# Attention weights transposed 64 rows at a time into two banks, with the first stage's order written anew

## What is computed

```python
x = x + xcond(layernorm(x), ctx, ctx, tau, delta, L0 weights)   # 16 heads of 32, 77 keys a batch
x = x + ffn(layernorm(x), ...)       # 512 -> 64, sum over relu(s*W1+b1)*W2, -> 512
x = x + xcond(layernorm(x), ctx, ctx, tau, delta, L1 weights)
x = x + routed_attention(x, ...)     # local windows, a router, attention of routed tokens

# xcond, for each batch and head
scores = q @ k.T * tau + delta       # 2048 x 77
a      = softmax(scale * scores)
out    = (a @ v) @ Wo.T + bo
```

## Time and profile before

| | us |
|---|---|
| median of 3 runs (3152.45 to 3153.17) | 3153.17 |
| the profiled execution | 3140.98 |
| its span, first to last instruction | 3139.1 |
| mean granted clock of PE, share of full speed | 0.985 |
| busy in the span: PE / weight loads | 3014.0 / 2391.9 |
| busy in the span: DVE / POOL / ACT | 2369.4 / 1781.6 / 1562.6 |

### The profile page before, as it was taken

One profiled execution on the slowest core, in us unless ns is written; L12 is line 12 of the kernel. 1 busy time (PEld: TensorE's weight loads), 2 busy tenths in 40 slices (PEclk: granted clock), 3 DMA queues, 4 the chain that ended last, 5 costly groups with the idle time before them and its releaser, 6 DMA issues.

```text
span 3139.1 us, 54652 instructions
## 1 busy us (share of the span) xinstructions
PE 3014.0 (96%) x21954; PEld 2391.9 (76%) x21954; DVE 2369.4 (75%) x3974; ACT 1562.6 (50%) x2605; POOL 1781.6 (57%) x1284
## 2 busy tenths in 40 slices
PE   7999999999999999999969999999999999988998
PEld 4777777777777888888847777777777777766886
DVE  4788888888898888888745776777878785566553
ACT  2575766666666666566533343433333333335443
POOL 1665656566658888899833454544455454575210
PEclk9999999999999999999979999999999999999999
DMA  4001010101111111111120111111122221132100
GB/s 161 34 30 55 28 57 28 56 28 61 47 58 71 47 52 57 51 57 38 68 84 18 65 58 55 55 63 51 60 91 81 85 81 58 44 134 65 34 18 11
DMA packets 87452, 180.18 MB, mean 57 GB/s; under 512 B 9526, under 2 KB 10294, under 8 KB 85664
## 3 DMA queue, kind: packets, MB, share of 16 engines
q1 hardware_dynamic: 82512, 161.73, 14.9%
q0 software_dynamic: 3968, 10.50, 1.1%
q10 hardware_dynamic: 720, 4.46, 0.3%
HBM read 106.05 MB, written 70.60 MB: 56 GB/s over the span
## 4 chain that ended last, share of the span: by engine, by line
PE 85%; DVE 8%; issue 3%; ACT 1%; POOL 1%; DMA 1%; SPq 0%; POOLq 0%; DVEq 0%; ACTq 0%
PE ps L264 17%; PE ps L266 16%; PE ps L265 16%; PE ps L271 7%; PE ps L489 6%; PE ps L479 5%; PE ps L259 4%; PE ps L1126 4%; PE ps L498 3%; PE ps L1146 3%; PE ps L1720 2%; DVE sTa L614 1%; PE ps L1703 1%; DVE Sb L634 1%; DVE xn L1204 1%
## 5 line engine op out<-in xcount | busy, mean ns | idle before, releaser
L824 POOL TENSOR_TENSOR Sb<-Sb,dn 128x1232 f32<-128x1232 f32 x128 | 288.5, 2254 | 226.7 <-DVE dn L649 226.7
L774 ACT COPY PT<-ps 77x512 f32<-77x512 f32 x512 | 289.3, 578 | 205.8 <-PE ps L489 204.2
L1533 POOL TENSOR_TENSOR Sw<-Sw,dw 128x1024 f32<-128x1024 f32 x128 | 242.3, 1894 | 234.5 <-DVE dw L1251 234.2
L1478 ACT COPY PU<-ps 128x512 f32<-128x512 f32 x256 | 141.4, 588 | 443.1 <-PE ps L271 442.1
L819 POOL TENSOR_TENSOR Sb<-Sb,mx 128x1232 f32<-128x1232 f32 x128 | 295.2, 2306 | 103.2 <-DVE mx L641 100.4
L489 PE MATMUL ps<-ident,Sb 128*77 128x128 f32 x2048 | 312.7, 279 | 0.9 <-ACT PT L774 0.5
L1528 POOL TENSOR_TENSOR Sw<-Sw,mw 128x1024 f32<-128x1024 f32 x128 | 243.3, 1901 | 122.3 <-DVE mw L1244 122.2
L489 PEld LDWEIGHTS ps<-ident,Sb 128*77 128x77 f32 x2048 | 240.9, 148 | 67.2 <-issue 42.6
L646 DVE TENSOR_REDUCE dn<-Sb 128x16 f32<-128x1232 f32 x128 | 183.5, 1434 | 72.4 <-ACT Sb L768 71.4
L1238 DVE TENSOR_TENSOR Sw<-ps,msk 128x1024 f32<-128x1024 f32 x128 | 155.6, 1216 | 107.3 <-PE ps L1126 107.2
L634 DVE TENSOR_TENSOR Sb<-ps,dlt 128x616 f32<-128x616 f32 x256 | 200.2, 782 | 38.6 <-PE ps L479 38.6
(11 more groups left out here) (276 smaller groups left out, 8087.9 us busy)
## 6 DMA issues: line engine op xcount, KB each, us to landing
XB<-in_x SPq DMA_DIRECT2D x16, 1024.0 KB, 5.5
x_scratch<-XB SPq DMA_DIRECT2D x16, 1024.0 KB, 4.6
XB<-x_scratch SPq DMA_DIRECT2D x16, 1024.0 KB, 5.8
x_scratch<-XB SPq DMA_DIRECT2D x64, 256.0 KB, 2.0
XL<-x_scratch SPq DMA_DIRECT2D x64, 256.0 KB, 3.1
XY<-x_scratch SPq DMA_DIRECT2D x64, 256.0 KB, 2.8
y_scratch<-XY SPq DMA_DIRECT2D x64, 256.0 KB, 2.0
out<-yo SPq DMA_DIRECT2D x64, 256.0 KB, 2.0
```

Source lines behind the costliest of these rows:

```text
L774: A.copy(PT[:, 4 * g:4 * g + 4, :], ps[0:NK, bank("PT", n, g), :].rearrange("p (c n) -> p c n", c=4)).then_inc(a_pt, 1)
L824: G.tensor_tensor(sv, sv, last(dn[:, n % 2, :], NK), ALU.mult).then_inc(g_norm, 1)
L1533: G.tensor_tensor(weights(n, p), weights(n, p), last(dw[:, n % 2, 4 * p:4 * p + 4], 256), ALU.mult).then_inc(bg_norm, 1)
```

## The change

`ptrans` now handles eight heads at once, in two row groups: for each head the upper 64 queries go to one bank and the lower 64 to the next, so that a head takes two transposes of 64 rows x 77 columns instead of one of 128 x 77. It fills the pair of banks 2 and 3, and there is one such pair. `Wo` moves from bank 2 to bank 4. `pcopy` copies both banks in one operation of 77 x 1024, twice for a tile instead of four times 77 x 512. The semaphore counts follow (two for a tile instead of four). All five tables of stage A have new numbers; in `TILE`, `ptrans` stands at 274 and 310 instead of 247, 263, 275 and 300, `scores` at 13 and 74 instead of 28 and 70.

```diff
-TILE = {"scores": (28, 70), "sadd": (-14, 54), "smax": (67,), "sub": (55,), "softexp": (124,), "den": (140,),
-        "norm": (115,), "ptrans": (247, 263, 275, 300), "pcopy": (222, 257, 289, 313), "pv": (329,), "ohi": (320,),
-        "olo": (325,), "wo": (381,), "xadd": (419,), "store": (415,)}
-LATE = {"xstat": (438,), "rsx": (436,), "zrow": (598,), "rmul": (608,), "route": (666,), "comb": (710,)}
-PREP = {"stats": (-431,), "aggr": (-415,), "rstd": (-414,), "ln": (-347, -310, -282, -239),
-        "bias": (-304, -274, -241, -130), "turn": (-273, -238, -217, -173), "xhi": (-283, -264, -188, -186),
-        "low": (-283, -248, -208, -183), "q": (-123, -64, -45, -27), "qcopy": (-110, -70, -66, -30)}
-FEED = {"stats": (719,), "aggr": (721,), "rstd": (698,), "ln": (753, 764, 812, 842), "bias": (701, 705, 887, 982),
-        "turn": (779, 824, 848, 912), "xhi": (783, 817, 834, 910), "low": (768, 837, 855, 875), "win": (949,),
-        "sT": (931,), "relu": (940, 987, 1022, 1031), "accu": (962, 982, 1034, 1038),
-        "wout": (1088, 1091, 1111, 1124), "fadd": (1044, 1048, 1061, 1065), "storeb": (977,)}
+TILE = {"scores": (13, 74), "sadd": (16, 57), "smax": (80,), "sub": (116,), "softexp": (121,), "den": (144,),
+        "norm": (207,), "ptrans": (274, 310), "pcopy": (258, 307), "pv": (341,), "ohi": (321,), "olo": (339,),
+        "wo": (402,), "xadd": (419,), "store": (601,)}
+LATE = {"xstat": (433,), "rsx": (496,), "zrow": (568,), "rmul": (664,), "route": (671,), "comb": (632,)}
+PREP = {"stats": (-406,), "aggr": (-397,), "rstd": (-361,), "ln": (-327, -310, -289, -220),
+        "bias": (-156, -110, -39, 63), "turn": (-283, -231, -202, -182), "xhi": (-292, -255, -211, -185),
+        "low": (-270, -247, -187, -182), "q": (-100, -63, -8, -7), "qcopy": (-137, -74, -64, -14)}
+FEED = {"stats": (730,), "aggr": (738,), "rstd": (749,), "ln": (744, 755, 800, 844), "bias": (749, 922, 968, 1008),
+        "turn": (799, 832, 888, 902), "xhi": (771, 813, 849, 900), "low": (786, 843, 870, 882), "win": (959,),
+        "sT": (922,), "relu": (953, 976, 1030, 1032), "accu": (968, 993, 1040, 1043),
+        "wout": (1103, 1107, 1111, 1112), "fadd": (1044, 1049, 1057, 1058), "storeb": (976,)}
...
-        pool_a = {"S": Banks((0,)), "PT": Banks((3, 4)), "PV": Banks((5,)), "Wo": Banks((2,))}
+        pool_a = {"S": Banks((0,)), "PT": Banks((2,)), "PV": Banks((5,)), "Wo": Banks((4,))}
...
-            def ptrans(n, g):
-                p = take("PT", n, g)
+            def ptrans(n, p):
+                s = take("PT", n, p)
                 pe.wait_ge(g_norm, n + 1)
-                for i in range(4):
-                    o = NK * (4 * g + i)
-                    m = PE.transpose(ps[0:NK, p, 128 * i:128 * i + 128], Sb[:, n % 3, o:o + NK], ident[:, :])
+                for i in range(8):
+                    o = NK * (8 * p + i)
+                    for r in (0, 1):
+                        k = slice(64 * r, 64 * r + 64)
+                        m = PE.transpose(ps[0:NK, s + r, 64 * i:64 * i + 64], Sb[k, n % 3, o:o + NK], ident[k, k])
                 m.then_inc(pe_pt, 1)
...
-            def pcopy(n, g):
-                ac.wait_ge(pe_pt, 4 * n + g + 1)
-                ac.wait_ge(pe_pv, 2 * (n - 1) + g // 2 + 1)
+            def pcopy(n, p):
+                s = bank("PT", n, p)
+                ac.wait_ge(pe_pt, 2 * n + p + 1)
+                ac.wait_ge(pe_pv, 2 * (n - 1) + p + 1)
                 ac.wait_ge(st_V, 128)
-                A.copy(PT[:, 4 * g:4 * g + 4, :],
-                       ps[0:NK, bank("PT", n, g), :].rearrange("p (c n) -> p c n", c=4)).then_inc(a_pt, 1)
+                A.copy(PT[:, 8 * p:8 * p + 8, :].rearrange("k h (r q) -> k r h q", r=2),
+                       ps[0:NK, s:s + 2, :].rearrange("k r (h q) -> k r h q", h=8)).then_inc(a_pt, 1)
```

More of the change, by code:

```diff
@@ L110, in order_a @@
+FIRST = {"keys0": (-1306, -1097, -986, -916), "vals0": (-697, -407, -397, -387), "dscale": (-842,),
+        "whi0": (-1080, -985, -891, -859, -854, -817, -719, -697, -616, -566, -543, -477),
+        "wlo0": (-1537, -1326, -1300, -1138, -1027, -954, -947, -905, -903, -887, -841, -530), "loadk": (-960,),
+        "loadv": (-311,), "fprep": (-540,), "b2": (-239,), "cfadd": (-250,), "keys1": (-387, -148, -130, 0),
+        "vals1": (35, 82, 139, 189)}
 def order_a():
@@ L377, in build @@
                  "S": lambda n, p: (v_sadd, 2 * n + p + 1),
-                 "PT": lambda n, g: (a_pt, 4 * n + g + 1),
+                 "PT": lambda n, p: (a_pt, 2 * n + p + 1),
                  "PV": lambda n: (v_olo, n + 1),
@@ L495, in pv @@
                 for h in range(16):
-                    pe.wait_ge(a_pt, 4 * n + h // 8 * 2 + 2)
+                    pe.wait_ge(a_pt, 2 * n + h // 8 + 1)
                     o = 32 * (h % 4)
@@ L630, in sadd @@
                 ve.wait_ge(pe_s, 2 * n + p + 1)
-                ve.wait_ge(pe_pt, 4 * (n - 2))
+                ve.wait_ge(pe_pt, 2 * (n - 2))
                 ve.wait_ge(v_init, 3)
@@ L1622, in build @@
         c_xt, c_q, c_k, c_v, c_sn = again((pe_xt[0], 2 * NT), (pe_q, 8 * NB), (pe_wout, NT), (pe_xt[1], NT), (pe_win, NB))
-        c_s, c_pt, c_pv, c_ot, c_wo = again((pe_s, 4 * NT), (pe_pt, 8 * NT), (pe_pv, 4 * NT), (g_norm, 2 * NT), (pe_wo, 2 * NT))
+        c_s, c_pt, c_pv, c_ot, c_wo = again((pe_s, 4 * NT), (pe_pt, 4 * NT), (pe_pv, 4 * NT), (g_norm, 2 * NT), (pe_wo, 2 * NT))
         cv_w, cv_xlo, cv_v, cv_sn, cv_nm = again((v_acc, 8 * NB), (v_xlo[0], 2 * NT), (a_kb, 32), (v_vx, NT), (v_max, 2 * NT))
@@ L1628, in build @@
         ca_w, ca_xhi, ca_q, ca_k, ca_exp = again((a_relu, 8 * NB), (a_xhi[0], 2 * NT), (a_q, 8 * NB), (a_st, NB), (a_exp, 2 * NT))
-        ca_pn, ca_pt, ca_ohi = again((a_zx, NT), (a_pt, 8 * NT), (a_ohi, 2 * NT))
+        ca_pn, ca_pt, ca_ohi = again((a_zx, NT), (a_pt, 4 * NT), (a_ohi, 2 * NT))
         cg_one, = sems("cg_one")
```

## The result

| | before | after |
|---|---|---|
| median of 15 runs each (us) | 3153.70 (3149.45 to 3156.52) | 3160.41 (3155.50 to 3163.34) |
| ratio, 95% interval | | 1.002 [1.0012, 1.0028] |
| the profiled execution's span | 3139.1 | 3159.4 |
| mean granted clock | 0.985 | 0.975 |
| stage A ends (start of the last `rmul`) | 1605.9 | 1613.2 |

I forecast 3119 us, 1.1% faster than before; measured were 3160.4 us, 0.2% slower. Of the 20.3 us between the two spans, 13.0 lie in stages B and C, which the change does not touch; over all profiled executions of this study these two took 1529 to 1548 us, whatever stage A was. What the change did is stage A's +7.3 us, and that agrees with the 6.7 us between the medians.

A forecast was written before the change was run, and what follows sets the result against it. PE was taken to bound the second half, PE and one DVE-led stretch the first. Savings of 17.6 (`ffn` blocks), 12.6 (router), 3 (first two) and 1 (start) made -34 us: 3107 profiled, 3119 median, range 3075 to 3156.

The forecast's parts named there:

- 9.64 + 0.60 = 10.24 us: First half: the stretch DVE leads before `scores` grows by one `low` of 0.60 us put ahead of `sadd`.
- The transposes: `ptrans`: row halves run side by side, 0.066 us a pair, eight heads in 0.53 us instead of 0.87.
- rival (a): Row halves of `ptrans` do not overlap as thought: 0.12 or 0.132 us a pair, 3184 or 3209 us; chance 0.12.
- PE alone: Second half: a block bounded only by PE's own work would take 39.2 us.
- The second half: Router blocks: period falls from 42.09 to 41.2 us, 0.9 less.
- the chain of DVE's steps as its leader: Second half: 19.2 us of DVE steps against some 16.3 of PE's work, so PE waits for `sadd`.
- that last term: Second half: `pv`'s ninth product waits 0.3 us for the `pcopy` copy once a block, where PE waits anyway.
- (b): DVE does not hold PE back: blocks at PE alone, 47.9 and 39.2 us, total 3046; chance 0.15.
- (c): ACT's two-bank copy comes late and eats the gain: 0.15 us at each of eight copies a block, 3150 us; chance 0.13.
- The forecast's sign: Whole kernel: faster 0.77, same 0.10, slower 0.13.
- the new places: Stage A order: `ptrans` set beside `scores`, so 64-row work avoids two changes of shape that would cost all its gain.

The follow-up runs named there:

- e1: Changed kernel with one `ptrans` group, in the stretch DVE leads, issued three times instead of once in each `ffn` block; ratio 0.9955 to the kernel before.
- e6: Changed kernel with a block's fourth `ln` moved from -220 to -233, ahead of `zrow` and `relu` on ACT; ratio 1.0026 to the kernel before.
- e10: Changed kernel with one `ptrans` group issued three times, the third `low` behind `sadd` and the fourth `ln` at -233; ratio 0.9928 to the kernel before.
- e5: Changed kernel with `xstat` moved behind `olo` on DVE (433 to 440), as the kernel before had it; ratio 1.0061 to the kernel before.
- e3: Kernel before with the new order (tables) alone, keeping its 128-row transposes; ratio 1.0097 to the kernel before.
- e4: Changed kernel with the old tables, so the new code alone; ratio 1.0011 to the kernel before.
- e2: Changed kernel with a block's third `low` moved back behind `sadd` on DVE (-187 to -183); ratio 0.9968 to the kernel before.

## Why the prediction was wrong

Stage A by stretches, with bounds at the starts of DVE's `olo` of tiles 8, 56, 72 and 120 and of the last `rmul`; forecast and measured are differences to the kernel before in us:

| stretch | forecast | after | e1 |
|---|---|---|---|
| start to tile 8 | -4 | -3.4 | -4.6 |
| first half, 12 blocks | -13.2 | +7.2 | -10.5 |
| change to the router, 4 blocks | -4.4 | +5.1 | -0.7 |
| second half, 12 blocks | -10.8 | -3.2 | -3.0 |
| the end | -1.8 | +1.6 | +1.7 |
| sum | -34 | +7.3 | -17.0 |

**The failed step** is "9.64 + 0.60 = 10.24 us": a longer wait of PE, priced at DVE's own 0.60 us and no more. Its times were nearly right: blocks without a slow stretch take 50.87 where I forecast 50.6, and the longer wait was foretold ("growing from 1.4 to about 2 to 3 us"; it is 1.7 and 0.4). What I did not ask is what a longer wait does to PE's clock. It brought the 1.2 GHz level, for 3.4 us (a block of 52.4) or 6.8 us (53.7), which is 1.5 and 2.9 us a block. After minus e1 shows it: 17.7 us in the first half, 5.8 in the change to the router, 24.3 in all. That is more than the 17.0 us that the change brings in e1. The forecast missed stage A by 41.3 us; the clock is 24.3 of them, and the other 17.0 are missing at the full clock too: 7.8 in the second half, 3.7 in the change to the router, 3.5 at the end, 2.7 in the first half, less 0.6 at the start. A hint was in the profile: the kernel before had two stretches of 3.4 us at 0.5, at 853.6 and 959.4 us, in the change to the router.

**The transposes** were right in kind and a little low in size: 0.60 to 0.61 us for eight heads, 0.075 a pair, against 0.53 and 0.066. That refutes my rival (a). The rule in the Trainium skill (TensorE: Matmul & The Clock Gate, "What overlaps and what doesn't"), that a weight load overlaps running matmuls only when the row group differs, gave an estimate of 0.95 us for them; this trace does not agree. The missed size costs 8 x 0.07 = 0.6 us a block, so PE alone needs 39.8 in the second half, not 39.2.

**The second half** came to 41.86 (forecast 41.2, before 42.12): 0.26 us less, not 0.9. The step that failed there is the chain of DVE's steps as its leader: 19.2 us of DVE against 16.3 of PE. `scores` wait for `sadd` nowhere. In place of it, by the window's waits over its eight blocks: 7.6 / 8 = 0.95 for `olo`, 4.5 / 8 = 0.56 for `ln`, and the rest, 41.86 - 39.8 - 1.5 = 0.5, inside `pv`. From its start to the next work it runs 1.01 us in two of a block's four places, as in all four of the kernel before, and 1.17 and 1.30 us in the other two, 0.45 us more a block, its ninth product behind the copy (1244.42 + 1.01). I had that last term at 0.3 and hidden. That the sum still came to a little less than before is in part luck: I counted a wait that is not there and left out three that are. Which of them leads is only partly settled: e6 and e10 show `ln` to be worth 0.21 to 0.28 us, e5 that taking `olo`'s away alone does not help. Why the block got longer in e5 stays open.

**The rivals.** (b), PE never held back, is refuted by the waits in the second half, 12.1 us in eight blocks, though none of them is the one for `sadd`. (c), the copy of two banks: it takes 1.00 us, and the wait that it brings inside `pv`, 0.45 us a block in the second half, is real but under half of the price I gave (1.2 us). The end stays open: from tile 120 to tile 124 it takes 47.1 us instead of 43.1; with e1 at 46.1 the clock is at most a part of it.

**The forecast's sign.** In the kernel as it ran the new order brought nothing that can be measured: e3 shows that the new tables cost +1.0% with the old transposes, and e4 that the new transposes with the old tables are at 1.001 [1.0002, 1.0020], against 1.002 [1.0012, 1.0028] for both. With the clock held the order may be worth something, 50.86 in e1 against 51.35 for e4's blocks without a slow stretch; the old tables with a fill were not run. I took the new places as the thing that pays for the changes of shape, and never priced them against old places with new code.

## What to carry to other kernels

When a change frees PE's time beside an engine that does not get faster, ask of each wait that grows not only how long it is but whether the granted clock holds behind it: read the clock by stretches of a few us, not its mean, and look in the kernel before for single slow stretches, which may show where it is already close. If it falls, shorten the wait (e2: 1.1 us a block); where another engine sets its length, redundant work for PE inside it can be worth more than it costs (here 1.2 us of it a block gave 1.5 back). And test code and order apart: the new order here was worse than the old one with the old code and no better with the new.

## What was not expected of the hardware

- The fall to 1.2 GHz came with waits of 1.7 and 0.4 us inside dense work, and stayed for 3.4 or 6.8 us (10.2 once, at 853.3 us) while PE was busy again (6.25 of 6.80 us).
- The mean share of idle does not tell it. After the change PE is idle for 19.7 of 472 us in the first half at 0.97, and for 15.3 of 399.9 us in the second, nearly the same share, at 1.00; there its two waits lie 29 us apart (1219.6 and 1248.3), not 4.
- Transposes alone, put into the wait, were enough to hold the granted clock at 1.00 (e1).
- A slow stretch costs less than half its length (6.8 us: 2.9; 3.4 us: 1.5). Half would be the loss of a PE that is busy all the time; that the difference comes out of PE's waits is my reading and not shown.
